# Two graph layers on one core: the hub tile attended inside the adjacency stream, the dense neighbour product cut into pieces between the last ranked tiles

## What is computed

```python
# layer 0: h = relu(layernorm(x))
H = h @ W.T + b;  s = H @ a_s;  r = H @ a_r
e = leaky_relu(A * s + A * r.T, 0.2)
x = x + softmax(where(A > 0, e, -9e15), axis=1) @ H
# layer 1: h = relu(layernorm(x))
out = maximum(adj @ (h @ weight) + bias, 0)
x = x + max over the neighbours j of each row of out[j]
```

## Time and profile before

| | us |
|---|---|
| median of 3 runs | 2841.61 (2839.66 to 2843.04) |
| the profiled execution, its own time | 2837.29 |
| its span, first to last instruction | 2828.0 |
| around the span | 9.3 |
| TensorE / VectorE / ScalarE / GpSimd busy | 964.4 / 1384.9 / 456.6 / 1573.5 |
| mean granted TensorE clock | 0.671 |

### The profile page before, as it was taken

How to read it: one execution, slowest core, us unless ns; L and a number is a source line. 1 busy time by engine, 2 the same in 40 slices (tenths; PEclk the granted TensorE clock), 3 DMA queues, 4 the chain that set the end, 5 groups by cost and what they waited for, 6 DMA issues and landing times.

```text
span 2828.0 us, 19388 instructions
## 1 busy us (share of the span) xinstructions
PE 964.4 (34%) x4534; PEld 538.6 (19%) x4534; DVE 1384.9 (49%) x3508; ACT 456.6 (16%) x1519; POOL 1573.5 (56%) x1616
## 2 busy tenths in 40 slices
PE   3764145516235545524539978400000000000000
PEld 1431133303123213323414433200000000000000
DVE  6888667855344534452355544444574345112211
ACT  1531145302123214523400000000000000000000
POOL 0002755443564655675364563677556757777776
PEclk8887577767667768656759988755555555555555
DMA  9999667788567789623431221252123211222221
GB/s 351 392 384 386 192 233 282 301 207 329 195 213 279 276 301 389 213 66 76 122 85 44 76 63 50 77 106 59 47 59 43 52 37 49 50 55 51 52 48 41
DMA packets 155986, 447.44 MB, mean 158 GB/s; under 512 B 34557, under 2 KB 81459, under 8 KB 122970
## 3 DMA queue, kind: packets, MB, share of 16 engines
q1 hardware_dynamic: 80506, 311.94, 29.3%
q0 software_dynamic: 53184, 114.44, 17.3%
q10 hardware_dynamic: 22176, 19.77, 2.2%
HBM read 408.06 MB, written 37.95 MB: 158 GB/s over the span
## 4 chain that ended last, share of the span: by engine, by line
PE 18%; issue 18%; POOL 18%; another core or an unknown queue 11%; DVE 10%; DVEq 7%; DMA 7%; ACT 6%; SPq 4%; ACTq 1%; POOLq 0%
POOL ring L661 14%; PE psV L1093 10%; DMA a_buf<-in_adj 6%; PE psV L920 3%; SPq L390 2%; DVE ring L1331 2%; SPq L403 2%; PE psH L976 1%; POOL out L667 1%; DVE a_buf L1488 1%; DVEq L1333 1%; ACT ring L764 1%; DVE a_buf L1498 1%; DVEq L1502 1%
## 5 line engine op out<-in xcount | busy, mean ns | idle before, releaser
L589 POOL DMA_INDIRECT ring<-h_table,srec x518 | 506.7, 978 | 297.8 <-issue 172.4
L661 POOL DMA_INDIRECT ring<-p_table,srec x545 | 537.4, 986 | 198.7 <-issue 165.0
L1331 DVE TENSOR_TENSOR ring<-ring 128x128 f32<-128x128 f32 (+8 forms) x306 | 147.1, 481 | 505.1 <-DMA ring<-p_table,srec 317.4
L920 PE MATMUL psV<-a_buf,bit_ident 128*128 128x512 bf16 x1024 | 313.6, 470 | 229.8 <-DMA a_buf<-in_adj 167.3
L976 PE MATMUL psH<-ring,ident 128*128 128x128 f32 x1036 | 166.5, 325 | 240.0 <-issue 108.1
L624 POOL DMA_INDIRECT ring<-y_table,srec x198 | 193.1, 975 | 62.4 <-issue 62.4
L1093 PE MATMUL psV<-rec_all,a_buf 128*128 128x512 bf16 x888 | 202.1, 385 | 23.8 <-issue 23.7
L1103 PE MATMUL psH<-ones_row,flag_col 128*1 128x1 f32 x2 | 0.2, 163 | 610.8 <-DVEq L1559 610.8
L976 PEld LDWEIGHTS psH<-ring,ident 128*128 128x128 f32 x1036 | 156.8, 237 | 255.4 <-issue 242.6
L920 PEld LDWEIGHTS psV<-a_buf,bit_ident 128*128 128x128 bf16 x1024 | 114.0, 114 | 412.7 <-issue 244.0
L764 ACT ACTIVATE ring<-ring,prob 128x128 f32<-128x128 f32 x433 | 131.8, 388 | 5.4 <-issue 3.9
(11 more groups left out here) (228 smaller groups left out, 2000.3 us busy)
## 6 DMA issues: line engine op xcount, KB each, us to landing
a_buf<-in_adj SPq DMA_DIRECT2D x256, 1024.0 KB
ring<-p_table,srec POOLq DMA_INDIRECT x545
ring<-h_table,srec POOLq DMA_INDIRECT x518
trec<-records ACTq DMA_DIRECT2D x63, 128.5 KB
packed<-wbuf ACTq DMA_DIRECT2D x28, 256.0 KB
a_buf<-packed SPq DMA_DIRECT2D x7, 1024.0 KB
h_table<-stage POOLq DMA_DIRECT2D x16, 258.0 KB, 8.1
a_buf<-r_row SPq DMA_DIRECT2D x1, 4096.0 KB
```

The source lines that it names most:

```text
L589: pool.indirect_dma_start(ring[:, A_AT[q] + j, :], None, h_table, bass.IndirectOffsetOnAxis(srec_u[g][:, i, LIST + j:LIST + j + 1], 0)).th ...
L661: pool.indirect_dma_start(ring[:, C_AT[n] + j, 0:D], None, p_table, bass.IndirectOffsetOnAxis(slot, 0)).then_inc(s_rows[n % BUFS], 16)
L920: last = pe.matmul(psV[n % 2][:, h * BANK:(h + 1) * BANK].rearrange("p (g n) -> p g n", n=P), bit_ident[:, k, :], rows[:, :, k, :], start= ...
L1331: dve.tensor_tensor(ring[:, at:at + h, 0:D], ring[:, at:at + h, 0:D], ring[:, at + n - h:at + n, 0:D], op)
```

## The change

- **Groups.** Five groups instead of four, the first of 14 tiles instead of 16: `[(12, 14, 24), (1, 11, 48), (26, 10, 24), (36, 16, 24), (52, 12, 16)]`. The steps in STEP begin at 16 instead of 18. The gathers of attention are 529 instead of 518; 68 of them (15 tiles) instead of 85 (18 tiles) belong to steps from 64 on.
- **Records.** `rank_group` scatters the records RANK_BEFORE[g] = 0, 0, 3, 1, 1 ranked tiles ahead of the group's first, and reads the lists back up to one tile ahead; the wait for them stays at the group's first tile.
- **The hub.** Tile 0 is streamed at step 35, not last. Its words are kept on chip, and in steps 36 to 54 it is attended in 16 chunks of 512 columns with a running maximum: `hub_scores` (10 VectorE instructions), `hub_exponents`, `hub_turn`, `hub_times_h`, `hub_add`, one chunk a step, in psF instead of psV.
- **The dense product.** 36 tiles instead of 28: 9 batches, 72 pieces (a piece is one block of one batch, again 24 matmuls and 8 unpacking instructions, unpacked in two halves into four half buffers). Each batch is done in two units, first blocks 1, 2, 3, 0 (and 4, 5), later the rest; four banks of psV instead of two; the sums of the first five batches are copied to SBUF (`kept`) and put back by one float32 matmul each. Pieces 0 to 19 stand in steps 64 to 75 (PIECES_AT), with 12 splits in steps 64, 65 and 71.
- **What follows from 36 tiles.** 28 ranked tiles gather y (150 gathers, 28 scatters), with the sums placed from piece 26 to piece 66. The maximum needs 657 gathers instead of 638 (each dense tile has one more slot), the hub's rounds are paced over 29 tiles instead of 22, and the segments stand at place 35.

```diff
-STREAM = [t for a, n, _ in GROUPS for t in range(a, a + n)] + [0]
+HUB_BEHIND = 3
+STREAM = [t for a, n, _ in GROUPS[:HUB_BEHIND] for t in range(a, a + n)] + [0] + [
+    t for a, n, _ in GROUPS[HUB_BEHIND:] for t in range(a, a + n)]
...
-DENSE = 28
-DENSE_FROM = 27
+DENSE = 36
+DENSE_FROM = 35
...
+RANK_BEFORE = [0, 0, 3, 1, 1]
...
-STEP = [18, 19, 20, 20, 21, 22, 22, 23, 24, 24, 25, 25, 26, 26, 27, 27, 34, 38, 40, 41, 42, 43, 44, 45, 46, 46,
+STEP = [16, 17, 18, 18, 19, 20, 20, 21, 22, 22, 23, 23, 24, 24, 32, 37, 38, 39, 40, 41, 42, 43, 45, 45, 46, 48,
...
+PIECES_AT = {64: 2, 65: 5, 66: 2, 67: 1, 68: 2, 69: 1, 70: 1, 71: 2, 72: 1, 73: 1, 74: 1, 75: 1}
+SPLITS_AT = {64: 4, 65: 4, 71: 4}
...
-    return [m for m in range(len(Y_SLOTS)) if min((sum(Y_SLOTS[:m + 1]) + m + 8) * 9 // 32, DENSE_BATCHES * BLOCKS - 1) == step]
+def sums_behind(piece):
+    return [m for m in range(len(Y_SLOTS)) if min(SUM_FROM + (sum(Y_SLOTS[:m + 1]) + m + 6) // 4, NP - 1) == piece]
...
-    ready = [sum(work) * min(sum(C_SLOTS[1:m + 2]) / sum(C_SLOTS[1:23]), 1) for m in (n - 1, n)]
+    ready = [sum(work) * min(sum(C_SLOTS[1:m + 2]) / sum(C_SLOTS[1:30]), 1) for m in (n - 1, n)]
...
             for q in range(NR):
-                if RANKED[q][1] == 0:
-                    rank_group(RANKED[q][0])
+                for g in range(len(GROUPS)):
+                    if q == BASE[g] - RANK_BEFORE[g]:
+                        rank_group(g)
+                    if q == BASE[g] - min(RANK_BEFORE[g], 1):
+                        reload_records(g)
+                    if q == BASE[g]:
+                        pool.wait_ge(s_srec, 16 * (g + 1))
                 gather_h(q)
...
+            def hub_row(c):
...
+                sp.dma_start(hub_r[c % 2], r_row[0:1, c * BANK:(c + 1) * BANK].to_broadcast([P, BANK])).then_inc(
+                    s_hubr[c % 2], 16)
...
+            def dense_piece(i):
+                u, c, b = PIECES[i]
+                out = psA[UNIT_BANK[u]]
+                again = u >= DENSE_BATCHES
...
+                if i == BEGIN[u] and again and c < KEPT:
+                    pe.wait_ge(s_relu, u - DENSE_BATCHES - 3)
+                    pe.wait_ge(s_kept, c + 1)
+                    pe.matmul(out, ident[:], kept[:, c, :], start=True, stop=False)
+                pe.wait_ge(s_split, 2 * BLOCK_ORDER.index(b) + 2)
+                for h in range(2):
+                    pe.wait_ge(s_bits, 2 * i + h + 1)
...
+                if n >= T:
+                    for i in range(PIECE_FROM[n], PIECE_FROM[n + 1]):
+                        dense_piece(i)
```

436 lines of the change are left out of this document (281 added, 155 removed), and 5 rows, old and new, of the table SLOTS.

## The result

The changed kernel takes 2975.7 us (median of 4 runs, 2971.2 to 2979.1) beside 2842.3 for the kernel before: 1.048 of it, with a 95% interval of 1.046 to 1.051. It is slower by 133 us; I had forecast 2769, faster by 72, and 2975.7 lies outside my range. Its profiled execution has a span of 2965.6 us.

A forecast was written before the change was run, and what follows sets the result against it. Each phase has its own bound: the ranked chain, the hub, TensorE, then GpSimd. The phases sum to 1752 + 1004 = 2756 us, 2765 with 9.3 around it, and 2769 as a median beside 2841.6; range 2689 to 2842.

The forecast's parts named there:

- Stream: Adjacency streaming to the last packing: 1163 to 1150 us, more GpSimd work (+44) against earlier ranking (-23) and fewer waits (-34).
- The wait for the ranks and that for the lists go: -34: Group 3 in the stream: gathers now cover GpSimd's waits for ranks (21.6), lists (6.0) and record writes, saving 34 us.
- rival B: Hub chunks cost the stream 2.5 us or more a step: 40 us, 2809; 80 if r's row is late; chance 0.09.
- Last ranked tiles: From the stream's end to the last scatter: 257 us to 233, as the hub leaves and 20 pieces come in.
- 20 for steps 64 and 65: Start of the last ranked tiles: 20 us for ranks, first loads of y and words, and first splits, without pieces.
- I take 7 for each of the 11 steps from 66, 77: Last ranked tiles: each bare step from 66 on takes 7 us, 77 in all, with pieces added separately.
- Rival A: All 20 pieces between ranked tiles run at half the clock, 10.4 us each: 71 us more, 2840; chance 0.12.
- Product: Dense product to the first gather of p: 413 us to 368, with 52 pieces left and slow stretches mostly kept.
- rival C: The product's slow stretches don't come back and the maximum's waits halve: -55 - 25, 2689; chance 0.20.
- Maximum: Gathers of p to the end: 995 us to 1004, 19 more gathers (+24) against shorter waits for VectorE (-15).
- D: Slow stretches come more often; about four and a half turn the sign, five give 2860; chance 0.09.
- E: Early pieces wait for splits of y, so time moves instead of falling: within 20 us of forecast, inside its 0.50.

The follow-up runs named there:

- late records: The changed kernel with each group's records scattered and read back at its first tile, as in the kernel before: 2983.1 us (1.045 of the kernel before).
- the unpacking ahead: The changed kernel with VectorE's unpacking of the next piece placed ahead of the step's scores: 2925.5 us (1.023 of the kernel before).

## Why the prediction was wrong, step by step

**Stream, -13 forecast, +119 measured.** On the chip of the second kind, where nothing else disturbs, the phase is +46, with the hub's chunks and the pauses in it. GpSimd sends 39 more indirect DMAs there before the last packing (537 instead of 498); at 1.25 us that is 49, and I had booked 44 for 35. So this term fits, and the two credits against it came to nothing. "The first group is ranked two steps earlier: -23" did happen (GpSimd's first record at 223 us instead of 247, the second group's at 494 instead of 521), but the second group's wait for ranks rose from 13.0 to 33.0 us, and at the run of gathers that began at 797 us before, and begins at 813 now, the lead is gone. "The wait for the ranks and that for the lists go: -34" is the step that was wrong in kind: I took a wait of GpSimd for time on the path. With pauses after 16 gathers that wait is 21.9 us on a chip of the first kind and under 1.5 on the second, so it came with the slowed engines; and with late records it is gone as well, and the time did not rise. Then the hub: booked at 0, 46 to 48 measured on the first kind. That is rival B at its price of 40, and for 27 us of it by the mechanism that I priced at 80 there, the row of r queued behind a 4 MB tile; I had given it 0.09 because I trusted VectorE's 56% and did not ask which wait ends last in those steps. The rest of the 119, about 30 us, stays open. I put it down to stretches in other places, of which I knew in one phase only, but no run shows it, and SyncE's loads of the stream are, summed in the same way as above, less late in the changed kernel (213 us) than before (276).

**Last ranked tiles, -24 forecast, +66 measured.** The pieces were sized well: 20 of them take 128 us on TensorE, I said 136, and at 6.4 us each they are in the 6 to 7 that I named. What failed stands around them, in two terms. The busy rows of the changed kernel for steps 64 and 65, and from 66 on:

```profile
1282.00:1419.00 137.00, 59.23 (x279) 33.81 (x277) 57.60 (x185) 29.74 (x122) 63.52 (x66) 0.70 0.31 77
1419.00:1602.00 183.00, 113.51 (x505) 57.94 (x506) 59.09 (x223) 39.47 (x160) 43.63 (x42) 0.80 0.17 47
```

The larger is "20 for steps 64 and 65". With their seven pieces these two steps take 137 us where my sum had 68: 69 of the 87 us by which the phase is over my sum. Without pieces they take 64, not 20. The first piece starts at 1338, 56 us after the last packing, behind the last extraction, its ranks (GpSimd waits 15.4 us for them, until 1315.9), the first loads of y and four splits. Between the second and the third piece are another 40 us: ScalarE's late copy, 20, then a tile's scores and four more splits. That is read from the traces; no experiment takes these steps apart.

The smaller is the overlap. "I take 7 for each of the 11 steps from 66, 77" with 13 pieces of 6.8 makes 165, and they took 183. I added the 7 us and the pieces, but left out what stands between them: the piece's bits are unpacked behind the scores, the scores wait for the turn behind the piece before, 4.8 us a step. With the unpacking ahead the same steps took 126, less than my sum. The 7 us themselves were low: the 4.7 and 7.7 us of the earlier trace rows were the shortest steps of the phase, those at its very end, and the late steps without pieces took 8 to 10. I named the test "wrong in the reasoning if the steps from 66 on last more than 20 us each"; from the first piece of step 66 on they lasted 11 to 25, 17 in the mean, against 15 in my sum. For steps 64 and 65, where most was lost, I had named none.

**Rival A, pieces at half clock.** Behind a gap the first twelve matmuls took 4.5 us (the piece from 1498.78) and the next twelve 2.75, so pieces came out at 6.4 us, between its 10.4 and the 5.2 of the long stretch. Behind no gap they took 5.1 to 5.4 us. The granted clock of this piece, its first and its second half:

```profile
1498.80:1503.30 4.50, 4.50 (x13) 1.66 (x14) 0.64 (x4) 0.00 (x0) 1.02 (x1) 0.60 0.14 29
1503.30:1506.00 2.70, 2.70 (x16) 1.43 (x14) 0.00 (x0) 0.00 (x0) 0.00 (x0) 1.00 0.00 0
```

It is 0.60 in the first, mostly the lower level (0.5, 1.2 GHz), and 1.00 in the second (2.4 GHz); in the kernel with the gaps closed it is 1.00 over the whole piece from 1447.79. The Trainium skill, page "TensorE: Matmul & The Clock Gate", section "Loop structure matters more than you think", shows a loop with a long wait for a DMA before every matmul as one in which the matmuls run cold. The trace agrees for the first half of a piece only; the waits here are 4.7 us, for VectorE, and ahead of 24 matmuls.

**Product, -44 forecast, -52 measured.** The term 52 x 24 x 0.216 stands. That the stretches come back, 55 us, stands too on the first kind (36 us from 1626 to 1662, 40 from 1794 to 1834); on the second kind, as in rival C, there are none and the product takes 288.

**Maximum, +9 forecast, +5 measured** (+17 on the second kind). Right.

**Rivals D and E.** D, stretches come more often, asked for two and a half more than the two in the product. There were two, as before. Its thought, that dense code moved under the work of all engines meets more of them, is borne out by ScalarE's 20 us in step 65 at most; in the stream nothing shows it. E, that the time only moves, doesn't cover a phase that grew by more than the product lost.

**The sign.** The last ranked tiles alone came out 86 and 90 us above my sum on the two kinds of chip, more than the 72 us of gain that I forecast. That carries the sign on both. The whole loss was 58 us on the second kind, with pauses in both kernels, and 133 to 142 on the first, without.

## What to carry to other kernels

A bare step of a phase is priced by the mean of the phase, with the work to be removed taken off, and not by its shortest steps, and its first steps, where ranks, first loads and first splits come together, by themselves; and where work is put between steps, its preparation on the other engine must stand ahead of the wait that the work itself prolongs. A wait in one engine's list is a credit only if nothing else was late at the same time. A small transfer that an engine needs at once must not be queued behind a tile of 4 MB.

## What the hardware showed

Chips differ by kind. The same kernel took 2839 to 2860 us in four groups on three chips (and 2842 in the first measurement) and 2495 on one. In the slower kind all engines but GpSimd fall into stretches in which an instruction comes every 0.7 or 1.4 us, 14 to 90 us long ahead of the last phase and 124 to 181 in it. Most of the former begin 15 to 30 indirect DMAs into a run that GpSimd issues at a pitch of 1.25 us, and end some 10 us behind it; but the longest run, of 298, had none. Such a stretch costs the product some 30 us, and pauses of 2 us after 16 gathers gave 1.1% on such a chip and cost 4.9% on the other. The DMA queues are not full in a stretch: in the one from 1626 to 1662 their share was 0.22.

```profile
1626.00:1662.00 36.00, 10.55 (x21) 2.06 (x20) 2.76 (x13) 0.60 (x1) 22.00 (x24) 0.54 0.22 46
1662.00:1790.00 128.00, 119.44 (x533) 52.77 (x532) 78.57 (x277) 0.00 (x0) 68.20 (x70) 0.96 0.22 60
```

TensorE runs 21 matmuls in 36 us of the first row and 533 in 128 of the second, with GpSimd busy by six and five tenths. TensorE is busy for 10.55 of the 36 us, at a granted clock of 0.54, and for 119.44 of the 128, at 0.96. The Trainium skill, page "Runtime: NRT & Kernel Launch", section "Instruction fetch mechanics", says that each engine fetches its instructions ahead by itself and that this is mostly hidden. The four traces of the second kind show nothing against it. In a stretch on the first kind an engine starts one instruction at a time (1.40 us apart at 692.96 us); that its instructions come late would fit, but no row shows the fetch itself. Whether GpSimd's DMAs do it at all, what in them does, and what sets the chips apart, stays open: a pause and a shift of TensorE's instructions were tried, and other pitches, queues or sizes of gather were not.
